# Attention over sorted edges: groups of 256 entries, a short last chunk, pad rows of their own, left blocks loaded by SP

## The reference

```python
h = jnp.maximum(_layernorm(x), 0.0)
ngl, ngr = h @ Wl.T, h @ Wr.T                   # 4 heads of 16
gl, gr = ngl[a], ngr[b]
score = (att * leaky_relu(gl + gr, 0.2)).sum(-1)
alpha = softmax of score over the entries that share a
out = segment_sum(gr * alpha, a)
x = x + (gelu(concat(out, h) @ W1.T + b1) @ W2.T + b2)
```

## Time and profile before

| | |
|---|---|
| median of 3 runs | 7814.7 us (7803.67 to 7849.53) |
| the profiled execution, own time | 7800.33 us |
| its span | 7798.3 us |
| POOL busy | 4792.4 us (61%) |
| DVE busy | 4676.7 us (60%) |
| PE busy | 3670.4 us (47%) |
| ACT busy | 740.8 us (9%) |
| HBM read, written | 467.39 MB, 117.55 MB |

### The profile page before, as it was taken

One profiled execution on the slowest core, in us unless ns is written; L12 is line 12 of the kernel. 1 busy time (PEld: TensorE's weight loads), 2 busy tenths in 40 slices (PEclk: granted clock), 3 DMA queues, 4 the chain that ended last, 5 costly groups with the idle time before them and its releaser, 6 DMA issues. The chain is left out here.

```text
span 7798.3 us, 61909 instructions
## 1 busy us (share of the span) xinstructions
PE 3670.4 (47%) x17059; PEld 3413.6 (44%) x17059; DVE 4676.7 (60%) x6878; ACT 740.8 (9%) x1160; POOL 4792.4 (61%) x4913
## 2 busy tenths in 40 slices
PE   2002123577677776777767777674811111222223
PEld 1001123566676666766667666673701111111112
DVE  8999983556666566665666656664533333334443
ACT  4001000000000000000000000000111111111111
POOL 0000017777777777777777777773077777777774
PEclk9985555555555555555555555555655555555555
DMA  2000013444444443444444444456122222222221
GB/s 34 0 0 0 0 38 87 102 111 112 99 126 111 109 112 100 125 111 109 113 101 123 111 110 112 102 113 58 46 62 53 51 52 50 52 49 49 49 49 30
DMA packets 530887, 589.51 MB, mean 76 GB/s; under 512 B 274062, under 2 KB 277262, under 8 KB 530274
## 3 DMA queue, kind: packets, MB, share of 16 engines
q10 hardware_dynamic: 305904, 360.15, 14.9%
q0 software_dynamic: 156672, 160.75, 13.5%
q1 hardware_dynamic: 67954, 64.51, 2.7%
HBM read 467.39 MB, written 117.55 MB: 75 GB/s over the span
## 5 line engine op out<-in xcount | busy, mean ns | idle before, releaser
L827 POOL DMA_INDIRECT rows<-gr_table,row_of x3328 | 3199.8, 961 | 1978.2 <-issue 1013.5
L848 PE MATMUL bank<-terms,hot_sum 128*128 128x68 f32 x6656 | 1517.9, 424 | 885.6 <-DVE acc L1007 882.0
L1309 POOL DMA_INDIRECT message<-h_table,src_sb x1568 | 1574.0, 1004 | 553.6 <-issue 477.5
L848 PEld LDWEIGHTS bank<-terms,hot_sum 128*128 128x128 f32 x6656 | 1453.1, 331 | 938.8 <-DVE acc L1007 934.9
L839 PE MATMUL bank<-gl_step,hot_t 128*128 128x64 f32 x6720 | 1520.2, 421 | 309.3 <-DVE hot_t L999 228.4
L839 PEld LDWEIGHTS bank<-gl_step,hot_t 128*128 128x128 f32 x6720 | 1481.5, 333 | 320.4 <-DVE hot_t L999 234.6
L1021 DVE TENSOR_TENSOR fore<-bank,rows 128x512 f32<-128x512 f32 x416 | 286.8, 689 | 1287.3 <-DMA rows<-gr_table,row_of 1287.3
L1330 PE MATMUL bank<-edge_parts,edge_hot 128*128 128x192 bf16 x1568 | 286.4, 364 | 1588.0 <-DVE edge_parts L1392 1588.0
L1330 PEld LDWEIGHTS bank<-edge_parts,edge_hot 128*128 128x128 bf16 x1568 | 202.8, 141 | 1671.4 <-DVE edge_parts L1392 1660.4
L1385 DVE TENSOR_TENSOR bank<-message,edge 128x512 f32<-128x512 f32 x196 | 139.2, 710 | 1001.0 <-DMA message<-h_table,src_sb 1001.0
L952 ACT ACTIVATE bank<-fore 128x512 f32<-128x512 f32 x416 | 250.2, 602 | 3609.2 <-DVE fore L1021 3410.3
(11 more groups left out here) (264 smaller groups left out, 2934.4 us busy)
## 6 DMA issues: line engine op xcount, KB each, us to landing
place_b<-place_rows ACTq DMA_DIRECT2D x422, 256.0 KB
gr_rows<-rows ACTq DMA_DIRECT2D x416, 256.0 KB, 2.0
rows_again<-gr_rows ACTq DMA_DIRECT2D x416, 256.0 KB
rows<-gr_table,row_of POOLq DMA_INDIRECT x3328
edge<-in_edge_attr SPq DMA_DIRECT2D x97, 512.0 KB, 3.7
gl_step<-gl_table ACTq DMA_DIRECT2D x844, 32.0 KB
message<-h_table,src_sb POOLq DMA_INDIRECT x1568, 2.4
pen_s<-pen_rows ACTq DMA_DIRECT2D x52, 64.0 KB, 2.1
```

The costliest lines, as they stand in the source:

```text
L827: pool.indirect_dma_start(rows[k][:, g, :], None, m.gr_table[:, :], bass.IndirectOffsetOnAxis(m.row_of[:, tile:tile + 1], 0)).then_inc(s_g ...
L848: last = pe.matmul(sums_of(r % SUM_SLOTS, g // GROUP_TILES), hot2[slot][:, g, :], by_tile[:, g, :], start=g % GROUP_TILES == 0, stop=g % G ...
L1309: pool.indirect_dma_start(rows[k][:, e, :], None, m.h2_table[:, :], bass.IndirectOffsetOnAxis(m.src[:, tile:tile + 1], 0)).then_inc(s_gath ...
```

## The change

- `GROUP_TILES` goes from 4 to 2 and `STEP_GROUPS` from 2 to 4: a step still has 8 tiles and 1024 entries, but four groups of 256, with four left blocks and four accumulates. Blocks are padded to multiples of 256.
- 403 steps instead of 416 (1612 groups, 3224 tiles instead of 3328): 12 chunks of 32 and one of 19. `turn_steps` spreads the 32 sums of chunk 11 over the 19 score steps of chunk 12. The scan keeps its size; the unused scores of the last chunk are set to -1e30.
- `gr_table` gets 128 rows more (block 49, zeros), and a pad in partition p gathers row 6272 + p.
- `load_left` moves from ACT's queue to SP's, which waits for `left` of step q - 8.
- `s_step` is split: `left` waits for `hot_t` and signals `s_left`, `scatter` waits for `hot_sum` and signals `s_sum`. DVE waits for `s_left` before L1021, for `s_sum` in `term_of` and in each `accumulate`. The accumulates of a step stand behind the terms, the larger-of, `hot_t` and `hot_sum`.
- The steps that loaded past the end (pads of `blk_i`, `place`, `row_of`) are gone.

```diff
-GROUP_TILES = 4
+GROUP_TILES = 2
...
-CHUNKS = 13
-GROUPS = 832
-STEP_GROUPS = 2
+STEP_GROUPS = 4
...
+SIZES = [32] * 12 + [19]
+CHUNKS = len(SIZES)
+START = [sum(SIZES[:c]) for c in range(CHUNKS + 1)]
+STEPS = START[CHUNKS]
+GROUPS = STEPS * STEP_GROUPS
...
-        m.gr_table = nc.dram_tensor("gr_table", (N, D), F32).ap()
+        m.gr_table = nc.dram_tensor("gr_table", ((BLOCKS + 1) * P, D), F32).ap()
...
-            half = GROUPS // 2
-            for i in range(2):
+            part = GROUPS // 4
+            for i in range(4):
...
+            c.link(dve.tensor_scalar(pad_row[:, :], m.iota_node[:, 0:1], float(BLOCKS * P), None, ALU.add))
-            c.link(dve.tensor_scalar(m.row_of[:, 0:TILES], pad_t, float(N - 1), None, ALU.min))
+            c.link(dve.tensor_scalar(m.row_of[:, :], pad_t, pad_row[:, :], None, ALU.min))
...
+    def turn_steps(c):
+        score, sums = (SIZES[c] if c < CHUNKS else 0), (SIZES[c - 1] if c else 0)
+        before = START[c - 1] if c else 0
+        if not score:
+            return [(None, [before + i]) for i in range(sums)]
+        return [(START[c] + i, list(range(before + i * sums // score, before + (i + 1) * sums // score)))
+                for i in range(score)]
...
+        @block.sync
+        def _(sp):
+            for q in range(STEPS):
+                at_least(sp, s_left, q - U + 1)
+                for i in range(STEP_GROUPS):
+                    blk = sp.value_load(m.blk_i[0:1, q * STEP_GROUPS + i:q * STEP_GROUPS + i + 1], min_val=0,
+                                        max_val=BLOCKS - 1)
+                    sp.dma_start(gl_s[q % U][:, i, :], m.gl_table[bass.ds(blk, 1), :, :].rearrange("b p f -> p (b f)")
+                                 ).then_inc(s_gl[q % U], 16)
...
-            def body(part, j, first):
-                for k in range(U):
-                    q = U * j + k
-                    if part.sum:
-                        pe.wait_ge(s_summed, q - CHUNK_STEPS + 1)
-                    else:
-                        pe.wait_ge(s_hot, q + LAG + 1)
-                    if part.score:
-                        last = left((k + LAG) % U, j + (k + LAG) // U + 1)
-                    if part.sum:
-                        last = scatter(q - CHUNK_STEPS, k % LAG)
-                    last.then_inc(s_step, 1)
...
+            for c in range(CHUNKS + 1):
+                for q, sums in turn_steps(c):
+                    if q is not None and q + LAG < STEPS:
+                        left(q + LAG)
+                    for r in sums:
+                        scatter(r)
+                if c < CHUNKS:
+                    scan(c)
...
+            def accumulate(r, groups):
+                for i in groups:
+                    g = r * STEP_GROUPS + i
+                    blk = dve.value_load(m.blk_i[0:1, g:g + 1], min_val=0, max_val=BLOCKS - 1)
+                    sums = m.acc[:, bass.ds(blk, 1), :].rearrange("p b f -> p (b f)")
+                    at_least(dve, s_acc, g)
+                    dve.wait_ge(s_sum, r + 1)
+                    dve.tensor_tensor(sums, sums, sums_of(r % SUM_SLOTS, i), ALU.add).then_inc(s_acc, 1)
...
+            def sum_step(r, base):
+                weight_of(r, base)
+                term_of(r)
+                if r - LAG >= base:
+                    accumulate(r - LAG, (0, 1))
+                hot_sum_of(r)
+                if r - LAG >= base:
+                    accumulate(r - LAG, (2, 3))
...
+                if c < CHUNKS and SIZES[c] < CHUNK_ROWS:
+                    dve.memset(scores[:, SIZES[c] * STEP_TILES:, :], -BIG)
+                for q, sums in turn_steps(c):
+                    if q is not None:
+                        score_step(q, c, sums[0] if sums else None, base)
+                        sums = sums[1:]
+                    for r in sums:
+                        sum_step(r, base)
```

More of the change, by code:

```diff
@@ L779, in attention, with loads @@
     HALF = ROW_TILES // 2
[L781 to L797, removed]
-            turn(Part(c))
+    def loads(q, slots):
+        return (q // slots + 1) * 16
+    def turn_steps(c):
[5 more added lines that the diff above has]
+                for i in range(score)]
     def sums_of(slot, i):
@@ L833, in _, with left @@
         @block.tensor
         def _(pe):
-            def left(slot, loads):
-                pe.wait_ge(s_gl[slot], loads * 16 * STEP_GROUPS)
+            def left(q):
+                pe.wait_ge(s_hot, q + 1)
+                pe.wait_ge(s_gl[q % U], loads(q, U) * STEP_GROUPS)
                 for g in range(STEP_TILES):
-                    last = pe.matmul(bank[slot % LAG][:, g * D:(g + 1) * D], hot_t[slot % LAG][:, g * P:(g + 1) * P],
-                                     gl_s[slot][:, g // GROUP_TILES, :], start=True, stop=True)
-                return last
@@ L843, in scatter @@
-            def scatter(r, slot):
+                    last = pe.matmul(bank[q % LAG][:, g * D:(g + 1) * D], hot_t[q % LAG][:, g * P:(g + 1) * P],
+                                     gl_s[q % U][:, g // GROUP_TILES, :], start=True, stop=True)
+                last.then_inc(s_left, 1)
+            def scatter(r):
+                pe.wait_ge(s_summed, r + 1)
                 at_least(pe, s_acc, STEP_GROUPS * (r - SUM_SLOTS + 1))
-                by_tile = terms[slot][:, :, :].rearrange("p (g h) w -> p g (h w)", h=HEADS)
+                by_tile = terms[r % LAG][:, :, :].rearrange("p (g h) w -> p g (h w)", h=HEADS)
@@ L865, in scan @@
-            def scan(part):
-                c = part.c
+                last.then_inc(s_sum, 1)
+            def scan(c):
                 pe.wait_ge(s_sorted, c + 1)
-                if part.sum:
-                    pe.wait_ge(s_acc, c * CHUNK_GROUPS)
+                if c:
+                    pe.wait_ge(s_acc, START[c] * STEP_GROUPS)
                 for g in range(ROW_TILES):
@@ L958, in turn, with scan @@
-            def turn(part):
-                c = part.c
-                loop(part, body)
-                if not part.score:
-                    return
-                for k in range(U):
-                    act.wait_ge(s_store[k], (c * outer + outer) * 16)
-                act.sem_inc(s_sp, 1)
-                for r in range(c * CHUNK_STEPS, c * CHUNK_STEPS + V):
+                load_place(q)
+            def scan(c):
+                for k in range(START[c + 1] - U, START[c + 1]):
+                    act.wait_ge(s_store[k % U], loads(k, U))
+                for r in range(START[c], START[c] + V):
```

293 lines of the change are left out of this document (131 added, 162 removed).

## The result

The changed kernel takes 7609.85 us, the median of 4 runs (7602.36 to 7640.73), against 7810.65 us for the kernel before (4 runs, 7803.67 to 7849.53): a ratio of 0.974 with a 95% interval of 0.9699 to 0.9782. The forecast was 7600 us with a range of 7565 to 7655. The profiled execution took 7608.22 us with a span of 7606.3 us. I therefore compare the attention stage in the profiles, one profile per kernel, and give times beside it.

What follows compares the result with a forecast made beforehand. POOL's gathers were taken to set the attention step (9.98 us). From step 383 on 335.7 us against 552.7 (-217.0), preparation +2, gave 7585.3 us profiled; with 14.4 us for the median, 7600 us, range 7565 to 7655.

Steps and rivals of the forecast that it cites:

- POOL sets the pace: Attention stage: POOL issues gathers without a stop, 9.98 us a step of eight; 13 steps fewer save 130 us.
- Pads: Last steps: pads gathering one row lose 71 us; with 128 rows their price is taken at nothing.
- Rival A: Pad steps stay slow although they fetch 128 rows: 7627 us, chance 0.08.
- Accumulates under cover: Score steps: two more accumulates cost nothing under POOL's 9.98 us; at a scan L1021 spacing grows 40.5 to 44.4 us.
- Left blocks on SP: Attention steps: SP issues 1612 loads, ACT loses two issues a step, off the path; worth nothing.
- The last chunk and the tail: From step 383 to the last accumulate: 335.7 us against 552.7; DVE sets the end, 9.4 us behind the gathers.
- rival B: Last chunk: the second scatter stands in line instead of beside DVE, 13 x 3.41 = 44 us: 7644 us, chance 0.08.
- preparation: Before the attention, with decode: two more matmuls and bank reads, longer arrays: +2 us, at most +5.
- the 14.4 us added for the median of the runs before: Whole kernel: the earlier median (7814.7 us) lay 14.4 us above the profiled execution, so 7585.3 became 7600 us.
- the signs: Profile checks: step 383 within 5 us of 5020.8, gather median 944 ns, no POOL waits, pad steps near 10 us.
- Rivals C and D: C: PE waits for SP's left blocks, about 8400 us, chance 0.04; D: an overlooked cover eats the gain, 7800, 0.02.
- The split of `s_step`: PE and DVE waits: left and scatter wait separately, PE starts left earlier; no gain.

Runs made afterwards that it cites:

- e10: The changed kernel with 416 steps again (13 chunks of 32): 7772.2 us, ratio 0.9958 to the kernel before.
- e5: The changed kernel with 13 even chunks of 31 steps instead of 12 of 32 and one of 19: 7627.7 us, ratio 0.979.
- e2: The kernel before with the 128 pad rows of the change alone: 7731.5 us, ratio 0.9899.
- e7: The kernel before with two pad rows, one for even and one for odd partitions: 7726.6 us, ratio 0.9898.
- e1: The changed kernel with all pads gathering the one row 6249 again: 7619.6 us, ratio 0.9747.
- e9: The changed kernel with the wait for scatter's matmuls once per call of accumulate, not before each: 7580.0 us, ratio 0.9718.
- e3: The changed kernel with its four left-block loads a step back on ACT's queue: 7620.5 us, ratio 0.9739.
- e8: The changed kernel with groups of 512, 405 steps in chunks of 11 x 32, 22, 16 and 15: 7572.1 us, ratio 0.9709.
- e11: The changed kernel with chunks of 10 x 32, 27, 22, 18, 16 and one scatter wait per accumulate call: 7565.8 us, ratio 0.968.

## Why the prediction was right, point by point

*POOL sets the pace.* Right: 3224 gathers, median 944 ns, no pause. The 13 steps less were costed at 130 us of gathering; e10 against e5 shows 135.8 with one sum alone (3.9) in it, so 132.

*Pads.* Priced at 71 us; e2 shows 73.8. That reads of one row are slow together and those of neighbouring rows are not, drawn from the place loads, stands (e7: two rows are enough). Rival A was priced at 27 us and e1, which brings it about, gives 20.0.

*Accumulates under cover.* Right in the 384 covered steps: z adds of settled steps keep POOL's pace, 9.98 us apart with 3.5 us of waiting left. The distance at a scan came to 45.1 to 45.8 us (44.4 forecast), since an accumulate takes 0.83 us, not 0.76. The step that failed was to carry over the duration of the earlier trace rows to a line that got one wait more; e9 shows that wait to be the whole difference. It costs 0.9 us at a scan and 7.7 us from step 383 on. The reason given for the 0.76 us, one accumulate waiting for the other, is not what the trace shows either: an accumulate is busy for 0.22 us. The rest is DVE's own stream, which reads the block's number and prepares the address before each; three of its operations in the changed kernel (ns min/median/max, first and last start in us):

```profile
L977 DVEq TENSOR_LOAD <-blk_i x1612: 296/303/969, 1510.8 to 5369.5; - x180
L977 DVEq FUSED_REGOPS  x1612: 183/183/210, 1511.4 to 5369.8; - x180
L980 DVEq EVENT_SEMAPHORE  x1611: 21/21/21, 1512.6 to 5370.1; - x179
```

The last starts of these fill the time up to the last accumulate (5370.27 us); the third row is the added wait, an operation of its own. And the 8.6 us read from the earlier trace rows for eight accumulates hold a wait for PE, ahead of the seventh:

```profile
5034.44 0.23 DVE L1007 TENSOR_TENSOR acc<-acc,bank 128x68 f32 x1 [3.14 <-PE bank L848]
```

Sixteen accumulates cover that wait. The forecast put a total in place of a total, so this did no harm; eight more accumulates at a scan cost 4.9 us, not 8 x 0.83.

*Left blocks on SP: "ACT loses two issues a step, off the path".* This is the term that was wrong. ACT's multiply stands between two of DVE's adds in every step. With four loads of 0.88 us ahead of it, DVE waits for it 1.9 to 3.7 us in every other step of the crowded chunk (e3). A paced step has 3.5 to 3.9 us of waiting for gathers to hide that, the crowded chunk has none. The move is worth 20.3 us, not nothing (e3). The total didn't suffer, because I summed the crowded chunk without any ACT time, which holds only with the loads on SP: the error is in what I credited the gain to.

*The last chunk and the tail.* From step 384 to 402: forecast 159.6 us, measured 161.9. DVE behind the gathers: forecast 9.4 us, measured 15.7 - 2.5 = 13.2. PE and DVE are level there, as supposed; PE's groups from 5078 to 5240 us in the changed kernel:

```profile
L846 PE MATMUL bank<-terms,hot_sum 128*128 128x68 f32 x448 | 101.1, 422 | 7.6 <-DVE acc L981 7.6
L836 PE MATMUL bank<-gl_step,hot_t 128*128 128x64 f32 x240 | 54.3, 421 | 4.9 <-DVE hot_t L970 4.9
```

The two overlap, and PE is busy for 149.5 of the 162 us, DVE for 139.9; PE's waits for DVE are 12.5 us in all, where rival B would need 44. Sums alone take 3.86 us a step, 3.93 with the few longer ones, not 4.16; the last two sets of accumulates 13 us, not 12.2. These cancel, which is luck: 338.1 us from step 383 on against the forecast's 335.7.

*Ahead of step 383 and behind the attention* three things weren't forecast: preparation +4.0 us instead of +2 (within the bound of 5), 7.6 us of stretched gathers, and 11.0 us behind the attention. With the 2.4 us from step 383 on they make up the 22.9 us between 7585.3 and 7608.22. On the medians the miss is 10 us, and that is partly luck: the 14.4 us added for the median of the runs before have no counterpart in the changed kernel, whose median lies 1.6 us above its profiled run. Of the signs, step 383 was to come within 5 us of 5020.8 and came 11.6 us late, and the later times (last scan, last accumulate) moved with it by 13 to 16 us; the gathers' median, POOL's waits, the spacing of the pad steps and the queue's share came as said.

*Rivals C and D* fell: PE waited for left blocks only at the start of the stage, and POOL waited 1.2 us. *The split of `s_step`*, put at nothing, was taken out alone by no run; its worth is open.

## What to carry to other kernels

Cost a cheap instruction by the place where it has no cover: ACT's issues and the accumulates' second wait cost nothing that shows in 384 paced steps, but 20 and 8 us in the last chunk and its tail, where each sum alone also cost 3.9 us. Ask what fills the time between two short operations: here it was reading an index, not the addition. The best edits here kept the end short and level (tapered chunks). When padding indices, spread them over a few addresses; one shared row turned 12 steps into a loss of 74 us. Two parts of a change can serve the same end: take each out alone from the changed kernel and add it alone to the old one, for the two prices differ (pads 74 and 20 us).

## What the hardware showed beyond that

*Gathers beside scans.* POOL's timeline in the changed kernel beside a scan, the gathers longer than 1.1 us:

```profile
4079.67 2.90 POOL L815 DMA_INDIRECT rows<-gr_table,row_of  x1 [0.30 <-issue]
4082.88 2.02 POOL L815 DMA_INDIRECT rows<-gr_table,row_of  x1 [0.30 <-issue]
4091.43 2.58 POOL L815 DMA_INDIRECT rows<-gr_table,row_of  x1 [0.30 <-issue]
4094.32 2.09 POOL L815 DMA_INDIRECT rows<-gr_table,row_of  x1 [0.31 <-issue]
```

DVE's timeline at the same time:

```profile
4079.53 2.29 DVE L1053 TENSOR_TENSOR_SCAN fore<-pen_s,score_s 128x1024 f32<-128x1024 bf16 x1
4081.86 2.29 DVE L1054 TENSOR_TENSOR_SCAN top<-pen_s,score_s 128x1024 f32<-128x1024 bf16 x1
...
4090.92 2.35 DVE L1090 TENSOR_TENSOR_SCAN fore<-pen_s,init,score_s 128x1024 f32<-128x1024 bf16 x1
4093.31 2.35 DVE L1091 TENSOR_TENSOR_SCAN top<-pen_s,init,score_s 128x1024 f32<-128x1024 bf16 x1
```

The long gathers are those that begin during one of the four long scans, and each of the 48 in the changed kernel ends 0.75 us (0.747 to 0.759) after that scan does. The first is 1.82 to 2.98 us, depending on where in the scan it begins, and this shifts with a few tenths of a us in DVE's steps: first gather to step 383 took between 3891.0 us (before) and 3906.2 (e3) in kernels with the same 3072 gathers and the same chunks up to there. The difference of the changed kernel, 7.6 us, is all in the long gathers: the idle time between the 3072 is 936 us in both. The Trainium skill, "SBUF — State Buffer", section "Who interferes with whom", has a rule for it: a DVE instruction with two SBUF inputs contends with a GpSimd instruction that reads SBUF, since its second input comes through a shared read interface. The trace agrees, with 4.7 to 5.9 us a chunk's scan; no run here took the scans away.

*Two clocks of the stage behind the attention.* From the last accumulate to the first gather of the messages it is 90.7 to 92.5 us in ten of the thirteen profiles and 131.3 us in three (e3, e8, e11). TensorE's granted clock in this stage (the column after the engines' busy times; then DMA share, GB/s), first in e9, with 91.9 us:

```profile
5356.00:5400.00 44.00, 33.21 (x161) 18.86 (x162) 16.18 (x11) 16.28 (x27) 15.24 (x3) 0.82 0.17 37
5400.00:5447.00 47.00, 17.39 (x89) 10.35 (x88) 21.54 (x19) 8.22 (x15) 0.00 (x0) 0.67 0.15 34
```

then in e8, with 131.3 us:

```profile
5344.00:5390.00 46.00, 34.66 (x93) 16.71 (x93) 15.12 (x9) 10.37 (x17) 15.10 (x3) 0.50 0.17 35
5390.00:5430.00 40.00, 40.00 (x116) 21.76 (x116) 2.53 (x6) 9.39 (x16) 0.00 (x0) 0.50 0.00 0
```

At 0.50, the lower of its two levels (1.2 GHz), PE stayed throughout in e8, as in e3 and e11; in e9 it had partly the upper one (2.4 GHz) from the first stretch on, as in the other nine. From 5000 to 5200 us, in the attention, both were granted 0.50, with PE busy for 162.7 and 169.2 of the 200 us. What decides between them stays open.
